# A decoder block on one core: the loads of the second loop's first groups, the late softplus, and the order around the tile table

## The reference, cut to what matters

```python
xn = layernorm(x, gamma, beta)
x_inner, z = split(xn @ W_in, 2)                 # 512 and 512 channels
x_conv = silu(causal_conv(x_inner, conv_w, 4) + conv_b)
xp = x_conv @ W_x                                # 16 of B, 16 of C, 1 of delta
delta = softplus(xp[:, :, -1:])
# h_t = exp(delta_t A) h_(t-1) + delta_t B_t x_t ;  y_t = C_t . h_t
y = (scan(x_conv, -exp(A_log), B, C, delta) + x_conv * D_skip) * silu(z)
x1 = layernorm(x + (y @ W_out + x))
x2 = layernorm(x1 + attention(x1, ctx))
out = layernorm(x2 + shared(x2) + experts(x2))   # 2 of 8 experts for each token
```

## Time and profile before

| | |
|---|---|
| median of three runs | 1718.99 us (1718.0 to 1720.59) |
| profiled execution, its own time | 1718.62 us |
| its span | 1716.8 us |
| TensorE matmul busy | 1645.8 us, 96% |
| VectorE busy | 1300.7 us, 76% |
| ScalarE busy | 946.6 us, 55% |
| GpSimd busy | 870.4 us, 51% |
| DMA | 240.79 MB, mean 140 GB/s |
| first loop | to about 252 us |
| second loop | from there to about 515 us |

### The profile page before, as it was taken

How to read it: one execution, slowest core, us unless ns; L and a number is a source line. 1 busy time by engine, 2 the same in 40 slices (tenths; PEclk the granted TensorE clock), 3 DMA queues, 4 the chain that set the end, 5 groups by cost and what they waited for, 6 DMA issues and landing times.

```text
span 1716.8 us, 38082 instructions
## 1 busy us (share of the span) xinstructions
PE 1645.8 (96%) x11304; PEld 1491.5 (87%) x11305; DVE 1300.7 (76%) x2688; ACT 946.6 (55%) x1643; POOL 870.4 (51%) x770
## 2 busy tenths in 40 slices
PE   7999986999998999999999998999999999999994
PEld 6777765989997888888888878999999999999994
DVE  7888867878885877777777777767777777777774
ACT  6788876778844334334334345555565565555552
POOL 1111125978962354354354363546666666666664
PEclk9999998999999999999999999999999999999997
DMA  4555556899954333332333344334445445445454
GB/s 151 191 190 190 190 193 212 242 267 268 268 219 149 117 125 103 116 130 101 118 130 101 116 151 120 58 63 101 99 100 112 94 99 116 95 96 115 96 104 104
DMA packets 149263, 240.79 MB, mean 140 GB/s; under 512 B 40960, under 2 KB 104640, under 8 KB 141008
## 3 DMA queue, kind: packets, MB, share of 16 engines
q1 hardware_dynamic: 122608, 203.58, 37.9%
q0 software_dynamic: 26592, 36.46, 11.9%
HBM read 132.30 MB, written 107.68 MB: 140 GB/s over the span
## 4 chain that ended last, share of the span: by engine, by line
PE 61%; DVE 3%; DMA 3%; issue 1%; POOL 0%; ACT 0%; another core or an unknown queue 0%; DVEq 0%; SPq 0%; ACTq 0%; POOLq 0%
PE block_banks L3094 22%; PE block_banks L3144 11%; PE block_banks L2985 5%; PE block_banks L2976 4%; PE block_banks L2899 4%; PE block_banks L2998 4%; PE block_banks L2920 2%; PE block_banks L3087 2%; PE block_banks L2931 2%; PE block_banks L2939 2%; PE block_banks L2887 1%; DMA attention_x<-x 1%; PE block_banks L2956 1%; DMA more<-back_y,back_token 1%; DMA attention_c_raw<-in_ctx_T 0%
## 5 line engine op out<-in xcount | busy, mean ns | idle before, releaser
L3094 PE MATMUL block_banks<-back_xe_T,back_w_split 128*128 128x256 f32 x3408 | 439.0, 285 | 1.5 <-DVE back_xe_T L2768 1.5
L3094 PEld LDWEIGHTS block_banks<-back_xe_T,back_w_split 128*128 128x128 f32 x3408 | 419.8, 193 | 1.9 <-issue 1.9
L2349 ACT ACTIVATE back_w_split<-back_w_gu 128x1024 fp32r x142 | 149.6, 1054 | 236.3 <-PE block_banks L3094 163.3
L3144 PE MATMUL block_banks<-back_w_down,back_he_T 128*128 x1680 | 213.1, 283 | 0.4 <-DVE back_w_down L2425 0.4
L2748 DVE TENSOR_TENSOR back_w_split<-back_w_gu,back_w_split 128x1024 fp32r<-128x1024 f32 x142 | 178.7, 1259 | 38.0 <-ACT back_w_split L2349 29.2
L3144 PEld LDWEIGHTS block_banks<-back_w_down,back_he_T 128*128 128x128 f32 x1680 | 206.6, 192 | 0.6 <-issue 0.6
L2185 POOL DMA_INDIRECT sorted<-back_x,back_slot x128 | 132.8, 1037 | 127.0 <-DVE back_slot L2571 79.8
L1582 PE MATMUL block_banks<-front_xn_T,front_w_in_parts 128*128 128x512 f32 x768 | 185.0, 396 | 2.5 <-DVE front_xn_T L1353 1.1
L1582 PEld LDWEIGHTS block_banks<-front_xn_T,front_w_in_parts 128*128 128x128 f32 x768 | 141.3, 188 | 39.7 <-DVE front_conv L1346 7.5
L2221 POOL DMA_INDIRECT acc<-back_y,back_token x71 | 112.3, 1581 | 120.4 <-DVE back_y L2787 115.4
L1346 DVE SCALAR_TENSOR_TENSOR front_conv<-block_banks,front_conv_wb,front_conv 128x508 f32<-128x508 f32 (+2 forms) x192 | 140.7, 740 | 33.3 <-ACT front_conv L1130 28.7
(11 more groups left out here) (290 smaller groups left out, 3480.4 us busy)
## 6 DMA issues: line engine op xcount, KB each, us to landing
back_xe<-sorted SPq DMA_DIRECT2D x72, 272.0 KB
gate_T<-front_gate_T SPq DMA_DIRECT2D x16, 1024.0 KB, 4.9
xc_T<-front_xc_T SPq DMA_DIRECT2D x16, 1024.0 KB, 5.8
front_xc_in<-xc_T SPq DMA_DIRECT2D x16, 1024.0 KB, 7.5
front_gate_in<-gate_T SPq DMA_DIRECT2D x16, 1024.0 KB, 6.0
front_c_rep<-c_parts SPq DMA_DIRECT2D x128, 64.0 KB, 5.4
front_rows_in<-in_x SPq DMA_DIRECT2D x16, 512.0 KB, 7.7
x<-front_x SPq DMA_DIRECT2D x16, 512.0 KB, 3.1
```

The lines of the kernel that those rows point to most:

```text
L2349: nc.scalar.activation(w_split[:, r, 0, m].unsqueeze(1), w_gu[:, bass.ds(e, 1), m], ACT.Copy).then_inc(w_high_ready, 1)
L3094: op = nc.tensor.matmul(dst[:, part, c % 2 * WINDOW:(c % 2 + 1) * WINDOW], w_split[:, r, w_part, m, k * D_FF + c * P:k * D_FF + (c + 1) * ...
L3144: op = nc.tensor.matmul(ps_y[:, s, 0:D_MODEL], he_T[:, r, h_part, k, seq(s)], w_down[:, bass.ds(e, 1), w_part, k], start=(n == 0), stop=(n ...
```

## The change

Front. SP's program no longer runs the first loop by `in_pairs`: pair 0 and pairs 1 to 5 are as before, pair 6 is written out with first=True, and `load_first(u)` stands in it; pair 7 has no `load_first`. Behind the loop SP waits for the stores of pairs 0 to 6 only, and for those of pair 7 at step 1. The store of delta moves from step 1 to step 14. VectorE does the last convolution of group 15 ahead of the wait for GpSimd's delta. The softplus of the last 8 sequences moves as a whole behind the chain of group 1 in step 0. TensorE's segments and the turn of delta for them move from step 0 to step 1, between the turned x of group 2 and the output product of group 0, with waits for ScalarE's emptied copies; delta is turned into bank 4 instead of 3. ScalarE's part moves from step 0 to the end of step 1.

Turn. In the step with the experts' group 14, `stats_of(a)` stands ahead of the rests of h 1 and 2. In the last one, `name_tiles` stands ahead of the rests of h 2 and 3.

```diff
--- before.py
+++ after.py
@@ -724,7 +724,7 @@
         ps_late, ps_early = ps[0:RANK, 6], ps[0:RANK, 7]
         ps_segment, ps_off = ps[:, 4:6].rearrange("p a b -> p (a b)"), ps[:, 7]
         ps_out_last = ps[:, 0:2].rearrange("p a (b c) -> p (a b) c", b=2)
-        ps_count, ps_delta = ps[0:1, 2, 0:1], ps[0:SEQS, 3, 0:T]
+        ps_count, ps_delta = ps[0:1, 2, 0:1], ps[0:SEQS, 4, 0:T]
 
         weights_loaded = sem("weights_loaded")
         w_in_loaded = sem("w_in_loaded")
@@ -920,7 +920,7 @@
                 load_gate(u, u)
                 load_rows(u, u)
 
-            def body(pair, last):
+            def body(pair, last, first=False):
                 for u in range(2):
                     g = 2 * pair + u
                     if not last:
@@ -931,17 +931,24 @@
                     if not is_at(g, 0):
                         store_xc(g - 1, 1 - u)
                         store_xp(g - 1, 1 - u)
-                    if last:
+                    if first:
                         load_first(u)
                     sp.wait_ge(gate_T_ready, KI * (g + 1) + 2)
                     sp.dma_start(d["gate_T"][g], gate_T[:, u]).then_inc(gate_stored[u], 16)
 
-            in_pairs(sp, body)
+            def groups_stored(pairs):
+                for stored, each in ((xc_stored, 16), (gate_stored, 16), (xp_stored, 32)):
+                    for u in range(2):
+                        sp.wait_ge(stored[u], each * pairs + 16)
+
+            body(0, False)
+            with sp.Fori(1, PAIRS - 2) as pair:
+                body(pair, False)
+            body(PAIRS - 2, False, True)
+            body(PAIRS - 1, True)
             store_xc(GROUPS - 1, 1)
             store_xp(GROUPS - 1, 1)
-            for stored, each in ((xc_stored, 16), (gate_stored, 16), (xp_stored, 32)):
-                for u in range(2):
-                    sp.wait_ge(stored[u], each * PAIRS + 16)
+            groups_stored(PAIRS - 1)
 
             same = None
 
@@ -951,9 +958,10 @@
                     sp.wait_ge(choice, CHOSEN)
                     same = sp.value_load(same_rows[0:1, 0:1], min_val=0, max_val=1)
                 if is_at(k, 1):
+                    groups_stored(PAIRS)
+                if is_at(k, LAST_GROUP - 1):
                     sp.wait_ge(delta_rows_ready, 1)
                     sp.dma_start(d["delta"].rearrange("(b t) -> b t", b=SEQS), delta_rows).then_inc(delta_stored, 16)
-                if is_at(k, LAST_GROUP - 1):
                     sp.wait_ge(x1_stored[0], 32)
                     begin.load_rows(sp)
                     for name in ("W_q", "W_k", "W_v"):
@@ -1302,7 +1310,7 @@
                     for s in range(GS):
                         nc.scalar.activation(x1[:, u, s], sum_rows[:, s], ACT.Identity, scale=rstd_1[:, s:s + 1],
                                              bias=shift_1[:, s:s + 1]).then_inc(x1_ready, 1)
-                if is_at(k, 0):
+                if is_at(k, 1):
                     segments(MOST, SEQS, 3)
                     act.wait_ge(delta_turned, 1)
                     nc.scalar.activation(delta_rows, ps_delta, ACT.Copy).then_inc(delta_rows_ready, 1)
@@ -1394,9 +1402,11 @@
                         statistics(g + 2, u)
                     convolve(g, u, 2)
                     if last and u:
+                        convolve(g, u, 3)
                         dve.wait_ge(chain_step, W_STEPS + RATIO + SERIES_POOL)
                         delta_parts_of(0, MOST)
-                    convolve(g, u, 3)
+                    else:
+                        convolve(g, u, 3)
 
             done = W_STEPS
 
@@ -1482,8 +1492,6 @@
                     if not early_group(k):
                         dve.wait_ge(out_done, k - 1)
                     add_skip(k, u, 0)
-                if is_at(k, 0):
-                    softplus_series(MOST, SEQS)
                 if there(k - 2):
                     g = k - 2
                     for s in range(GS):
@@ -1495,10 +1503,6 @@
                         nc.vector.bn_aggr(mean_1[:, s], stats_1[:, s]).then_inc(mean_1_ready, 1)
                 if there(k):
                     add_skip(k, u, 2)
-                if is_at(k, 0):
-                    softplus_end(MOST, SEQS)
-                    delta_parts_of(MOST, SEQS)
-                    all_steps(MOST, SEQS)
                 if is_at(k, LAST_GROUP):
                     begin.low_of(dve, "W_q", 0)
                     begin.low_of(dve, "W_k", 0)
@@ -1535,6 +1539,11 @@
                 if is_at(k, -1):
                     steps_by_pool()
                     softplus_ratio(MOST, SEQS)
+                if is_at(k, 0):
+                    softplus_series(MOST, SEQS)
+                    softplus_end(MOST, SEQS)
+                    delta_parts_of(MOST, SEQS)
+                    all_steps(MOST, SEQS)
                 if there(k - 1):
                     g, ug = k - 1, 1 - u
                     dve.wait_ge(out_done, g + 1)
@@ -1705,8 +1714,6 @@
                     count_rows()
                 if is_at(k, 0):
                     pe.wait_ge(choice, 5)
-                if is_at(k, 1):
-                    pe.wait_ge(delta_rows_ready, 1)
                 if is_at(k, LAST_GROUP):
                     pe.wait_ge(dx_ready, GS * GROUPS)
                     begin.turn_rows(pe, 0, False)
@@ -1722,6 +1729,14 @@
                 if is_at(k, LAST_GROUP + 1):
                     pe.wait_ge(skip_added, KI * GROUPS)
                     begin.project(pe, "W_q", 0)
+                if is_at(k, 1):
+                    pe.wait_ge(steps_ready, 2)
+                    pe.wait_ge(segment_ready, 2)
+                    segments(MOST, SEQS)
+                    pe.wait_ge(chain_step, W_STEPS + 2 * RATIO + SERIES_POOL + SERIES)
+                    nc.tensor.transpose(ps_delta, delta, ident).then_inc(delta_turned, 1)
+                    pe.wait_ge(segment_ready, 3)
+                    pe.wait_ge(delta_rows_ready, 1)
                 if there(k - 1):
                     g, ug = k - 1, 1 - u
                     out = ps_out_last if is_at(g, LAST_GROUP) else ps_out
@@ -1735,20 +1750,12 @@
                             op = nc.tensor.matmul(out[:, s], y_T[:, ug, j, seq(s)], w_out[:, j], start=(j == 0),
                                                   stop=(j == KI - 1))
                     op.then_inc(out_done, 1)
-                if is_at(k, 0):
-                    pe.wait_ge(steps_ready, 2)
-                    pe.wait_ge(segment_ready, 2)
-                    segments(MOST, SEQS)
                 if there(k + 2) and not is_at(k, -2):
                     g = k + 2
                     pe.wait_ge(late_exp, g)
                     late_sums(g)
                     pe.wait_ge(products_ready, g)
                     early_sums(g)
-                if is_at(k, 0):
-                    pe.wait_ge(chain_step, W_STEPS + 2 * RATIO + SERIES_POOL + SERIES)
-                    pe.wait_ge(skip_added, KI)
-                    nc.tensor.transpose(ps_delta, delta, ident).then_inc(delta_turned, 1)
                 if is_at(k, LAST_GROUP + 1):
                     begin.project(pe, "W_k", 0)
                     pe.wait_ge(sum_ready, 2 * LAST_GROUP)
@@ -2706,14 +2713,15 @@
                     hidden(g, 2, ahead)
                 if attention:
                     sum_rows_of(a)
+                if near_end:
+                    stats_of(a)
                 if expert and attention:
                     rest_h_s(g, 1)
                     rest_h_s(g, 2)
-                if near_end:
-                    stats_of(a)
                 if expert:
                     hidden(g, 3, ahead)
                     if not attention:
+                        name_tiles()
                         rest_h_s(g, 2)
                         rest_h_s(g, 3)
                 if near_end:
@@ -2722,7 +2730,6 @@
                     stats_of(a, g if expert else None)
                 if expert:
                     if not attention:
-                        name_tiles()
                         w_down_low(2)
                 if expert and attention and not near_end:
                     pick(g, u, second=False)
```

## The result

The changed kernel takes 1726.8 us (median of six, 1725.1 to 1731.3) where the kernel before, measured beside it, takes 1719.8: ratio 1.0044, 95% interval 1.0033 to 1.0055, so 7.6 us slower (5.7 to 9.5). The forecast was 1728.0, within 1720.5 to 1735.0. It was 1718.99 + 9.0. The kernel before came out 0.8 us longer this time, so the two should be compared by the difference: 9.0 forecast, 7.6 measured. The profiled execution took 1725.05 us and has a span of 1723.2 us. One of the nine executions of the experiment "between the stores" took 5357.8 us and is left out of its ratio.

The account below looks back on a forecast made before the run. TensorE was taken as the bound, without slack in either loop but with gaps between them. Stall +12.0, clock +2.5, between the loops -4.5 and tile table -1.0 gave +9.0 on 1718.99: 1728.0 us, range 1720.5 to 1735.

Parts of the forecast that it names:

- The rows behind the loads: First loop, pair 6: x_rows of group 15 queues behind load_first(0), lands at 224.4, stalling VectorE and TensorE: +12.0 us.
- The queue model: SP's queue: transfers land in order, so group 15's 0.52 MB waits behind 3.5 MB and lands 1.4 us after the gate store.
- The clock: After the first-loop stall: TensorE restarts at a lower clock, +2.5 us for group 14's first projections, bounds 1 and 5.
- Other queues past the loads: First loop: gate stores of groups 12 and 13 land late, near 223 and 245, but add no stall for ScalarE.
- Between the loops: From the first loop's end to the first L1735: convolution and softplus moves together gain 4.5 us, bounds 3 and 6.5.
- What was to be paid back: Between the loops: part of the 7.5 us gain lost again to the moved softplus, segments and ScalarE's order, leaving 4.5.
- The reason given for xc_in: Between the loops: loading groups 0 and 1 earlier frees SP to ask for group 2's xc_in near 271, landing near 277.
- "2.5 us" for the convolution: End of first loop: the last three convolution steps, run within the wait for delta, gain 2.5 us of TensorE's 4.46 gap.
- The turn: End of attention and expert steps: the earlier tile table gains 1.0 us, bounds -2.5 and +1; moved statistics gain 0.
- The sentence on the loops: Both loops: TensorE has no idle time of its own, so a delay to its next piece moves the end one for one.
- The sum: Whole kernel: +12.0 +2.5 -4.5 -1.0 = +9.0 us on the median, 1728.0 us; chance 0.72.
- The largest term: First loop: TensorE's stall behind the late x_rows of group 15, +12.0 us, bounds 4.4 and 15.

Follow-up runs that it names:

- e2: Kernel before with load_first moved from pair 7 to pair 6 and nothing else: 1729.5 us, ratio 1.0056.
- e3: Changed kernel with name_tiles and stats_of back in their old places at the turn: 1726.7 us, ratio 1.0046.
- e7: Kernel before with only the last three convolution steps of group 15 put ahead of the wait for delta: 1718.6 us, ratio 1.0006.
- e10: Kernel before with the last convolution ahead of the delta wait, and SP's wait for the stores of groups 14 and 15 moved to group 3's loads: 1715.6 us.
- e1: Changed kernel with load_first back in the last pair, pair 7, all else as changed: 1712.4 us, ratio 0.9960.
- e5: Changed kernel with load_first(0) in group 13 and load_first(1) in group 14, one group later: 1711.8 us, ratio 0.9969.
- e6: Changed kernel with load_first in the last pair, between the stores of xc and xp: 1712.3 us, ratio 0.9966.

## Why the prediction was right, and where it was not

**The rows behind the loads: right, a little too large.** Forecast: issue near 211.2, landing 224.4, VectorE stopped 12.0 us, TensorE as long. Found, less the 1.5 us by which this trace starts late: issue 211.0, the statistics at 223.2, VectorE stopped 10.7 us, TensorE 10.3. The queue model (3.5 MB ahead of 0.52 MB) gave the landing to about a microsecond; the term should have been 10.3. What was too large is the landing of the gate store in front of the rows: taken as 223.0, with the longest landing of the kernel before, found at 221.9. The 1.4 us for the rows behind it were right, 1.3 found (223.35 to 224.66). The runs with the rows first and one group later show that it is the order: the same bytes, 9.3 and 12.9 us less. The Trainium skill, DMA: Bandwidth & Descriptors, Queues, rings and completion order, has each DMA engine take the descriptors of one ring in order; the trace agrees with that (12.2 us of landing against a median of 5.5, and the six transfers landing in their order).

**The clock: right.** +2.5 forecast, 2.6 found (12.9 of delay less 10.3 idle), with a granted 0.50 as TensorE came back. The forecast was a choice within 1 to 5 us, so that it came so near is partly luck.

**Other queues past the loads: right for the change, wrong as a general size.** No wait for either gate store, as said, and the store of group 13 went out at 233.62, 232.1 less the late start (forecast 232), and landed at 244.78, 243.3 (forecast 245). The reason given, that the first stall covers the second, is what the kernel with the rows first shows: there ScalarE waits 4.0 us.

**Between the loops: the sum right, terms and reason not.** -4.5 forecast, -4.5 found. To compare with the trace of before, 14.35 us, the delay at the end of the first loop, are taken off. The early sums that wait for the products of group 1 were to start 7 us sooner; it was 5.5 (292.59 less 14.35 = 278.2 against 283.75). TensorE's next products were to start 7.5 sooner; it was 6.3 (279.2 against 285.52). VectorE began that chain as forecast (284.82 less 14.35 = 270.5, against 270.9), but it took 7.8 us and not 5.9: its two large multiplications took 2.16 and 2.17 us instead of 1.22 and 1.23 beside GpSimd (below). What was to be paid back, 3 us, was 1.8. The errors cancel, and that is luck. The prediction's list of TensorE's gaps was not complete either: it leaves out 3.48 us at 265.52 for ScalarE's scaling (L1259) and 3.77 us at 278.02 for the steps of the last 8 sequences (L1457), both in the trace of before. The second is gone after the change, since those segments moved.

The reason given for xc_in was half wrong. I wrote that the early loads let SP ask for it in time, and read SP's 13 us of standing from 261 to 274 us only in passing. The split of its wait does it alone: with the loads in their old place and the split, xc_in is out at 277.12 and TensorE doesn't wait for it; without the split it waits 7.0 us. The part of the diff that I had given no price, because the early loads seemed to do its work (they too free SP: 1.7 us in the kernel with the loads alone), is worth 11 us in a kernel with the loads back. And "2.5 us" for the convolution holds only with it: alone the convolution gains nothing that the times show.

**The turn: right within its bounds.** -1.0 forecast with -2.5 to +1. In the trace of the change it is 2.8 us sooner as read, which would be outside, and 1.3 with the accident taken off; 1 to 3 over all traces, and not to be told from nothing in the times. That VectorE's 1.88 us of idle time was the table's input arriving late was one of my readings; in the four other kernels with the old order (e2, e3, e7, e10) VectorE doesn't idle there at all, so it was most likely an accident of one execution. What the new order costs, 0.79 us of TensorE for the late rest of h, stands in all eight traces that have it.

**The sentence on the loops was too strong.** I wrote that TensorE has no idle time of its own in either loop. In the second it has some: single waits for xc_in of 0.3 to 2.4 us, at other groups in each trace (1.98 at 348.94 before). After:

```profile
473.29 1.09 PE L1679 MATMUL block_banks<-attention_ident,front_xc_in 128*128 128x128 f32 x8 [1.84 <-DMA front_xc_in<-xc_T]
```

I call them scatter because their groups and sizes differ between traces of like kernels. In the trace of before the DMA engines are 92% busy from 310 to 480 us, which leaves a load little room to come late; that this is the reason isn't shown. From 309.4 to 1010.7 us they move the delay between -1.3 and +2.6 us from kernel to kernel, with no relation to what was changed. That is a scatter which the forecast had no term for, and it limits what one trace can prove.

**The sum.** +9.0 us forecast, 7.6 measured (5.7 to 9.5). The mechanism, its place and the sign of every term that shows in the times are right. The largest term was 1.7 us too large, and the traces' scatter in the second loop, which no term stood for, added 0.8.

**What stays open.** By the times the loads alone cost 9.6 us (7.6 to 11.7), the rest of the diff alone gains 6.9 (4.6 to 9.1), and together they cost 7.6 (5.7 to 9.5), where the sum would be 2.7. By the traces up to the first output product the three are 11.0, 3.5 and 8.4 us: nearly additive. Part of the difference in the times is the gain that the early loads and the split share (SP free sooner, 1.7 us in e2); the rest may lie in the loops' scatter. No run here tells these apart.

The version that beats both is the change without its first part: 1711.8 to 1712.4 us in three forms (e1, e5, e6), 0.3 to 0.4% under the kernel before and 0.8% under the change.

## What to carry to other kernels

A prefetch issued earlier is free only if nothing that somebody waits for soon stands behind it in the same queue: list the issues behind it, with their consumers' due times, before moving it. A gap that two causes end is worth nothing to whoever removes one: here the convolution gave 0 us alone, with the split wait 2.6, and undoing the split turned a gain of 7 us into a loss of 4.5. When an engine's queue stands still for 13 us on one wait, ask which of its next instructions need that wait; only those should be behind it.

## What the runs showed of the hardware

Small VectorE operations that start while GpSimd works can last until GpSimd's operation ends. Timeline of VectorE after; those of 128x8 elements take 0.16 to 0.20 us when GpSimd is idle:

```profile
277.21 1.18 DVE L1422 TENSOR_SCALAR front_soft<-front_soft 128x8 f32<-128x8 f32 x1
278.42 0.20 DVE L1423 RECIPROCAL front_soft<-front_soft 128x8 f32<-128x8 f32 x1
278.66 1.14 DVE L1424 TENSOR_TENSOR front_soft<-front_soft 128x8 f32<-128x8 f32 x1
279.83 1.19 DVE L1425 TENSOR_TENSOR front_soft<-front_soft 128x8 f32<-128x8 f32 x1
281.06 0.17 DVE L1426 TENSOR_SCALAR front_soft<-front_soft 128x8 f32<-128x8 f32 x1
...
284.82 2.16 DVE L1524 TENSOR_TENSOR front_inner<-front_inner,front_c_rep 128x1024 f32<-128x1024 f32 x1
287.02 2.17 DVE L1526 TENSOR_TENSOR front_inner<-front_inner,front_xp_rows 128x1024 f32<-128x1024 f32 x1
```

GpSimd, same kernel, same stretch:

```profile
276.04 2.31 POOL L1065 TENSOR_TENSOR front_inner<-front_segment,front_a_bc 128x1024 f32<-128x1024 f32 x1 [4.49 <-DVE front_inside L1529]
278.50 1.28 POOL L1084 TENSOR_TENSOR front_late<-front_late,front_late_rep 112x512 f32<-112x512 f32 x1
279.74 1.26 POOL L1086 TENSOR_TENSOR front_early<-front_early,front_early_rep 112x512 f32<-112x512 f32 x1
282.16 5.95 POOL L1074 TENSOR_TENSOR front_y_T<-front_y_T,front_gate_in 128x512 f32<-128x512 f32 x4 [1.16 <-DVE front_y_T L1486]
```

The three long ones end at 278.39, 279.80 and 281.02; GpSimd's operations beside them end at 278.35, 279.78 and 281.00. The RECIPROCAL, which started 0.08 us ahead of GpSimd's next one, was not stretched. So a 0.17 us operation cost 1.1 to 1.2 here, and the multiplication that took 1.22 before took 2.16. Moving work on VectorE therefore changes its price by what GpSimd does at the new place: these five tiny operations cost 3.9 us, where the same five took 1.9 before (1.17 + 0.20 + 3 x 0.17, from 265.55). The Trainium skill, SBUF — State Buffer, SBUF: two separate sides, describes an exclusive lock on a port pair shared by the two engines, which whoever starts first holds for its whole instruction; ends that coincide within 0.04 us are what that would give.

An issue can hold SP much longer than its usual 0.43 us when many transfers are under way: one copy of late_rep took 4.50 us to issue in the changed kernel, with 4 MB asked for ahead of it and not yet landed (gate_in, the second loop's rows, a gate store, the rows of group 15 and a store of xc_T).

```profile
216.09 4.50 SPq L905 DMA_DIRECT2D front_late_rep<-xp  x1
```
